# Value matmuls of two key tiles side by side in layer 1's attention loop

## The reference, cut to what matters

```python
q, k, v = proj(query, w_q, b_q), proj(key, w_k, b_k), proj(value, w_v, b_v)
scores = einsum('bhqd,bhkd->bhqk', q, k) / sqrt(DK)
scores = where(mask == 0, -1e9, scores)
attn = softmax(scores, axis=-1)
x = einsum('bhqk,bhkd->bhqd', attn, v)
x = x.transpose(0, 2, 1, 3).reshape(b, -1, H * DK)
return x @ w_out.T + b_out
```

## Time and profile before

| what | us |
| --- | --- |
| median of 3 runs | 256.22 (256.07 to 256.94) |
| the profiled execution's own time | 256.07 |
| its span, first to last instruction | 254.2 |
| PE busy in the span | 224.8 (88%) |
| DVE busy | 186.6 (73%) |
| ACT busy | 155.4 (61%) |
| POOL busy | 79.5 (31%) |

### The profile page before, as it was taken

How to read it: one execution, slowest core, us unless ns; L and a number is a source line. 1 busy time by engine, 2 the same in 40 slices (tenths; PEclk the granted TensorE clock), 3 DMA queues, 4 the chain that set the end, 5 groups by cost and what they waited for, 6 DMA issues and landing times.

```text
span 254.2 us, 5091 instructions
## 1 busy us (share of the span) xinstructions
PE 224.8 (88%) x1644; PEld 137.0 (54%) x1656; DVE 186.6 (73%) x578; ACT 155.4 (61%) x225; POOL 79.5 (31%) x228
## 2 busy tenths in 40 slices
PE   3879899999999999989898789999988989989870
PEld 1464444445444448977686444455444447767760
DVE  7779876777676385678657897888775657789864
ACT  6775897565964762342223458777766674796570
POOL 4571346365522100100201153444412043344421
PEclk9999999999999999999999999999999999999999
DMA  6878799900110028800042683300000000000000
GB/s 212 275 214 173 208 137 182 339 26 26 40 62 3 0 62 161 152 3 0 0 124 65 217 280 96 95 4 0 4 0 3 0 0 4 1 0 3 0 21 22
DMA packets 18180, 20.41 MB, mean 80 GB/s; under 512 B 1553, under 2 KB 15609, under 8 KB 17825
## 3 DMA queue, kind: packets, MB, share of 16 engines
q1 hardware_dynamic: 17578, 19.16, 29.0%
q10 hardware_dynamic: 576, 0.94, 1.2%
HBM read 15.90 MB, written 4.19 MB: 79 GB/s over the span
## 4 chain that ended last, share of the span: by engine, by line
PE 57%; DVE 22%; issue 8%; DMA 4%; ACT 3%; POOL 2%; SPq 1%; DVEq 1%; POOLq 0%; ACTq 0%
PE bank L376 11%; PE bank L451 10%; PE bank L429 9%; PE bank L425 4%; DVE st L1061 4%; PE bank L549 3%; PE bank L550 3%; PE bank L569 3%; DVE row_max L875 3%; PE bank L624 2%; ACT q_stack L1370 2%; PE bank L382 2%; DVE shared_area L1099 2%; DMA aw<-in_attn_w 1%; PE bank L589 1%
## 5 line engine op out<-in xcount | busy, mean ns | idle before, releaser
L1385 ACT ACTIVATE probs<-bank 128x1024 f32<-128x1024 f32 x64 | 64.3, 1023 | 14.1 <-PE bank L429 9.0
L872 DVE CUSTOM_DVE_ANT_0 discard<-bank,bias_q 128x512 bf16<-128x512 f32 x64 | 43.3, 690 | 17.0 <-PE bank L376 15.3
L376 PE MATMUL bank<-k_stack,q_stack 72*128 72x512 bf16 x128 | 48.4, 384 | 4.1 <-DVE row_max L875 1.5
L875 DVE TENSOR_REDUCE row_max<-bank 128x1 f32<-128x512 f32 x64 | 42.0, 687 | 9.2 <-PE bank L376 6.7
L429 PE MATMUL bank<-q_stack,k_stack 102*128 102x256 bf16 x256 | 43.7, 272 | 1.1 <-ACT probs L1385 0.3
L451 PE MATMUL bank<-probs,v_ext 128*32 128x256 f32 x512 | 40.3, 391 | 0.2 <-ACT o_sb L1392 0.2
L1370 ACT COPY q_stack<-bank 6x512 bf16<-6x512 bf16 x32 | 18.5, 577 | 27.0 <-PE bank L398 26.9
L429 PEld LDWEIGHTS bank<-q_stack,k_stack 102*128 102x128 bf16 x256 | 24.8, 98 | 17.1 <-issue 1.4
L1626 POOL CAST max_part<-row_max 128x4 bf16<-128x4 f32 x32 | 6.2, 194 | 78.2 <-DVE row_max L875 44.4
L376 PEld LDWEIGHTS bank<-k_stack,q_stack 72*128 72x128 bf16 x128 | 12.3, 96 | 27.2 <-issue 11.9
L1433 ACT ACTIVATE early<-bank 128x512 f32<-128x512 f32 x12 | 7.1, 595 | 23.2 <-PE bank L550 23.2
(11 more groups left out here) (191 smaller groups left out, 362.5 us busy)
## 6 DMA issues: line engine op xcount, KB each, us to landing
k_stack<-k_bounce SPq DMA_DIRECT2D x9, 384.0 KB
q_bounce<-q_part SPq DMA_DIRECT2D x12, 192.0 KB, 3.0
k_bounce<-early SPq DMA_DIRECT2D x4, 384.0 KB, 3.0
experts_w<-in_wu SPq DMA_DIRECT2D x1, 1024.0 KB, 4.8
early<-in_wu SPq DMA_DIRECT2D x1, 1024.0 KB, 7.0
experts_w<-in_wg SPq DMA_DIRECT2D x1, 816.0 KB, 13.2
experts_w<-in_wu SPq DMA_DIRECT2D x1, 816.0 KB, 15.5
experts_w<-in_wd SPq DMA_DIRECT2D x1, 768.0 KB, 16.2
```

Source lines behind the costliest of these rows:

```text
L376: mm(bank[:, qt, :], q_stack[0:STACK, b, h, qt * 128:(qt + 1) * 128], k_stack[0:STACK, b, h, :], start=True, stop=True).then_inc(for_max, 1)
L872: ins = dve.tensor_tensor_reduce(discard[:, qt, :], bank[:, qt, :], bias_q[:, qt, :], 1.0, LOWEST, ALU.add, ALU.max, o)
L875: ins = dve.tensor_reduce(o, bank[:, qt, :], AX.X, ALU.max)
L1385: act.activation(probs[:, n % (2 * HG), :], bank[:, at:at + 2, :].rearrange("p a n -> p (a n)"), ACT.Exp, scale=SCALE).then_inc(exp_done, 1)
```

## The change

It has two parts, for layer 1 only (`l == 0`):

- PE: in the steps in which a group's block 0 or 2 stands (the odd ones), block kt and block kt + 1 are issued one behind the other; the even steps have none. The blocks are the same matmuls.
- ACT: `o_copy` of a group is in step 11 + 4g (`PV_LAG + 2`) and no longer in 12 + 4g. `o_transpose` and `divide` stay in steps 14 + 4g and 15 + 4g.

For layer 2 the constants give the same steps as before, and one block in each.

```diff
+OUT_COPY_STEP = (PV_LAG + 2, PV_LAG + 3)
+OUT_TURN_STEP = (PV_LAG + 5, PV_LAG + 5)
...
+        def group_of(s, first):
+
+            return (s - first) // HG if s >= first and (s - first) % HG == 0 else None
+
...
-                    if s % HG == (PV_LAG + 1) % HG and s >= PV_LAG + HG:
-                        o_transpose(l * B * NG + (s - PV_LAG) // HG - 1)
-                    if s >= PV_LAG:
-                        values(l * B * NG + (s - PV_LAG) // HG, (s - PV_LAG) % HG)
+                    if group_of(s, OUT_TURN_STEP[l]) in range(B * NG - 1):
+                        o_transpose(l * B * NG + group_of(s, OUT_TURN_STEP[l]))
+                    first = (s - PV_LAG) % HG
+                    for kt in ((first,) if l == 1 else (first, first + 1) if first % 2 == 0 else ()):
+                        if s >= PV_LAG:
+                            values(l * B * NG + (s - PV_LAG) // HG, kt)
...
-                    if s % HG == (PV_LAG + 2) % HG and s > PV_LAG + HG:
-                        divide(l * B * NG + (s - PV_LAG) // HG - 1)
+                    if group_of(s - 1, OUT_TURN_STEP[l]) in range(B * NG - 1):
+                        divide(l * B * NG + group_of(s - 1, OUT_TURN_STEP[l]))
...
-                    if s % HG == (PV_LAG - 1) % HG and s >= PV_LAG:
-                        o_copy(l * B * NG + (s - PV_LAG) // HG)
+                    if group_of(s, OUT_COPY_STEP[l]) in range(B * NG):
+                        o_copy(l * B * NG + group_of(s, OUT_COPY_STEP[l]))
```

## The result

| what | before | after |
| --- | --- | --- |
| median | 256.61 us (256.07 to 259.88, 14 runs) | 253.62 us (253.15 to 255.72, 14 runs) |
| ratio to before, 95% interval | | 0.9888 (0.9855 to 0.9921) |
| the profiled execution's own time | 256.07 | 255.72 |
| its span | 254.2 | 253.9 |

What follows compares the result with a forecast made beforehand. PE was taken to bound the kernel, busy 8.34 of 8.40 us per four loop steps. Terms 1.76 - 0.20 + 0.27 + 0.96 = 2.79, taken as 2.7, gave 253.4 us, median 253.5; range 252.8 to 255.5.

Steps and rivals of the forecast that it cites:

- Steps 9/10: Layer 1's loop, first pair of steps: no gain, since step 11's column scores wait for an exponential on ACT.
- Eight pairs, less the MISC wait: Steps 11/12 to 25/26: eight pairs save 1.76 us; waiting for MISC in steps 15, 19, 23, 27 costs 0.2.
- The range for the MISC wait: Steps 15, 19, 23, 27: `max_transpose` waits 0 to 0.2 us for the division to free MISC; 0.05 taken, four times.
- the third rival: `max_transpose` waits for the division in steps 15, 19, 23, 27, 31; MISC becomes the bound, 257.2 us; slower: chance 0.07.
- Steps 27 to 31 (terms 4 and 5): Steps 27 to 30 save 0.27 us, as blocks had covered waits; steps 30 and 31 nothing, DVE's chain decides.
- Steps 32 to 40: Loop's end: saves 0.96 us, by step 32's block under DVE's chain, two pairs and a covered wait, less two exponential waits.
- nothing on the path: ACT's copy of OUT, moved ahead of the even head's exponential, takes 0.37 us and fits in ACT's idle time.
- Carrying through: After layer 1's loop: the gain reaches the end whole; layer 2 costs and saves nothing.
- the first (a switch is not what costs): 0.57 us is the block's own price, so pairs save nothing: 256.2 us; no change: chance 0.11.
- The second rival (DVE in the even steps): Even steps each wait 0.1 us for maxima, 12 steps lose 1.2: 254.7 us; half lost to DVE or MISC: chance 0.20.

Runs made afterwards that it cites:

- e9_turn_early: The change, with group 6's OUT transposition moved from step 38 to 37 and ACT's cast of `sel` halved into steps 22 and 26: 253.32 us, ratio 0.9849.
- e5_layer2_too: The change, with paired blocks and the earlier copy of OUT in layer 2's loop too: 255.47 us, ratio 0.9957 to before.
- e6_five_groups: The change, with pairs for the first five groups only, single blocks from step 29, copy back in step 12 + 4g: 254.84 us in one run.
- e1_copy_back: The change, with ACT's copy of OUT back in step 12 + 4g and the pairs kept: 254.75 us, ratio 0.988 to before.
- second profile: The change run again without edit, for a profile without the clock dip: 254.0 us, ratio 0.9873 to before, span 251.7 us.
- e7_extra_alone: The change plus one extra block standing alone in each of steps 12, 16, 20 and 24: stretch from step 9's `max_transpose` to first full expert matmul 61.33 us.
- e8_extra_beside: The change plus four extra blocks directly ahead of the pairs in steps 13, 17, 21, 25: step 9's `max_transpose` to first full expert matmul 60.36 us.
- e4_four: The change, with all four blocks of a group together in one step and the copy in step 12 + 4g: 259.5 us in one run.
- e3_even_pairs: The change, with pairs in even instead of odd steps and the copy in step 12 + 4g: 256.65 us, ratio 0.9999 to before.

## Why the prediction was right

The mechanism and the sum held: 2.79 in S forecast, 2.83 measured. That the median came within 0.1 of 253.5 is partly luck: the kernel before read 256.61 in this comparison and not the 256.22 that the forecast starts from, and the medians lie 3.0 apart and not 2.7. In the sum, too, small misses cancel. By its own terms:

1. **Steps 9/10**, 0 forecast: 4.34 became 4.35. The exponential does set the pace there.
2. **Eight pairs, less the MISC wait**, 1.76 - 0.20 = 1.56 forecast: 33.58 became 31.92, 1.66. A plain pair saves 0.24 to 0.25 (4.09 to 3.84; 0.23 forecast), one with the transposition 0.20 (4.31 to 4.11), of which the MISC wait has taken 0.04 (54.63 to 54.89). The exception is the pair of steps 25 and 26, 0.08 for 0.21: the cast of `sel` on ACT makes the exponential late by which the column scores at 69.81 are released. I had looked at ACT's queue in steps 16 to 18 only, and `e9_turn_early` shows what it hid (4.11 again).
3. **The range for the MISC wait** was 0 to 0.2, and 0.05 taken: it is 0.04 to 0.05 in steps 15, 19 and 23 and nothing in step 27. In step 31, where DVE is behind, it is 0.41 (79.94 to 80.57), beneath DVE's chain, where it costs nothing; the third rival had counted this step with the others. `e5_layer2_too` shows the same mechanism with a price in layer 2.
4. **Steps 27 to 31 (terms 4 and 5)**, 0.27 forecast: 11.19 became 10.99, 0.20. Steps 27 and 28 gave 0.35 (4.62 became 4.27) for 0.39, and the pair in step 29 cost 0.15 for 0.12: `e6_five_groups` gives 0.14 more without it, since DVE's chain, which starts with the projection in step 29, is what ends last.
5. **Steps 32 to 40**, 0.96 forecast: 12.47 became 11.49, 0.98. The two waits for exponentials that were subtracted are there (0.20 in step 33, 83.92 to 84.32 for 0.20; 0.25 ahead of 91.02), and `e1_copy_back` shows that 0.71 of this term needs the copy on ACT in its new place; the prediction had given the move of the copy no worth of its own. It said "nothing on the path", which is true of what the copy costs, and overlooks what the old place would cost with pairs.
6. **Carrying through**: from the first full expert matmul to the end 158.80 before and 158.86 after (second profile). The gain arrives whole.

Of the rivals the first (a switch is not what costs) falls by the 0.97 us between `e7_extra_alone` and `e8_extra_beside`. The Trainium skill's "TensorE: Matmul & The Clock Gate", section "Step-by-step: what each phase is for", has weight loads pulled ahead of running matmuls; behind a block the trace shows them 0.41 us idle and at the very start of their matmul, after as before. The Trainium skill's "TensorEngine Tiling (Array Packing)", section "Key Properties", which says that a mode change drains the engine, is the rule with which these runs agree; 0.14 for leaving and 0.09 to 0.10 for entering are this case's measurements. Why the switch takes that long, and how it divides between drain and weight load, no run here separates. The second rival (DVE in the even steps) did not come: PE's rows of steps 11 to 27 wait for no maximum. With still shorter steps it came, in `e4_four`.

Of my expectations three were far off. `e4_four` (64.21 for 59.5 to 60.5) and `e3_even_pairs` (61.14 for 60.0) missed at the loop's end, by pricing an uncovered wait at what a block had left of it or not at all; `e4_four` also left out DVE's maxima in its short steps. `e5_layer2_too` (1.8 above the change for 0.5) left out the handover of MISC.

## What to carry to other kernels

Where TensorE alternates between column-tiled and full-width matmuls, count the changes between the two as well as the matmuls: here each pair of changes costs 0.23 us, half as much as the tiled work in between, and grouping two takes it off. Group only as far as the other engines keep up in the steps that become shorter, and look at whether the work moved had covered a wait: its length uncovered, from start to start, is the price. When a producer finishes earlier, move its consumer too (the copy here: nothing in the middle, 0.97 us where ACT or the next group is late), and judge by stretches between fixed marks, which repeat to 0.02 us where totals of one kernel scatter by one to four.

## What was not expected of the hardware

- The price of a switch is the same wherever it stands: 0.57 alone, 1.00 to 1.01 for two, 1.43 to 1.44 for three, 1.86 to 1.87 for four blocks, wherever the next matmul has nothing else to wait for, in each kernel above.
- The granted clock was 0.50 for some 3 us in one execution, between layer 1's loop and layer 2's, and 1.00 in another of the same kernel with the same work on PE ahead of it (1.01 and 1.54 of 2 us busy in both). It cost 1.6 to 1.7 us, more than half of what the change brings. What made the one fall and the other not stays open.
